# Moving the weight averages, one centring and one PSUM copy in a fused attention and convolution kernel

## The reference

```python
x = attention0(x)     # 1x1 projections q, k, v; softmax over 256 positions; gamma * out + x
x = attention1(x)     # the same form without the output projection
# layer 2: a pre-activation residual block with binary weights
out = relu(batch_norm(x, gamma0, beta0));  out = conv3x3(out, E0 * sign(w0))
out = relu(batch_norm(out, gamma1, beta1)); out = conv3x3(out, E1 * sign(w1)) + x
# layer 3: whitening across 4 groups of channels, then a 4x4 mix per channel
cov = perm @ perm.T / N + eps;  z = solve(cholesky(cov).T, perm);  y = weight @ z + bias
```

## Time and profile before

| | us |
|---|---|
| median of 3 runs | 70.65 |
| lowest and highest | 70.19, 70.87 |
| the profiled execution | 70.66 |
| its span, first to last instruction | 68.9 |

### The profile page before, as it was taken

One profiled execution on the slowest core, in us unless ns is written; L12 is line 12 of the kernel. 1 busy time (PEld: TensorE's weight loads), 2 busy tenths in 40 slices (PEclk: granted clock), 3 DMA queues, 4 the chain that ended last, 5 costly groups with the idle time before them and its releaser, 6 DMA issues.

```text
span 68.9 us, 1828 instructions
## 1 busy us (share of the span) xinstructions
PE 58.2 (85%) x654; PEld 34.6 (50%) x654; DVE 47.4 (69%) x129; ACT 43.0 (62%) x133; POOL 21.9 (32%) x59
## 2 busy tenths in 40 slices
PE   5997866839999899989695899979998999999910
PEld 2253531416364364445261457358974998774300
DVE  0029799487796987878699754677949969377440
ACT  0710498939989898989999593464008672455440
POOL 4001606860371817355303317470004050008200
PEclk9999999999999999999999999999999999999999
DMA  0889830000000000000000000000000000000025
GB/s 0 237 255 275 274 149 6 0 0 0 0 0 0 10 5 0 0 0 5 0 0 0 5 10 0 0 0 10 0 0 0 0 10 10 0 0 0 0 102 202
DMA packets 2168, 2.69 MB, mean 39 GB/s; under 512 B 368, under 2 KB 1520, under 8 KB 2160
## 3 DMA queue, kind: packets, MB, share of 16 engines
q1 hardware_dynamic: 1872, 2.39, 10.9%
q10 hardware_dynamic: 288, 0.20, 0.9%
HBM read 2.06 MB, written 0.52 MB: 37 GB/s over the span
## 4 chain that ended last, share of the span: by engine, by line
PE 54%; ACT 12%; DVE 11%; POOL 11%; issue 5%; POOLq 1%; DVEq 0%; ACTq 0%
PE bank L760 13%; PE bank L690 9%; ACT bank L458 8%; PE bank L590 6%; PE bank L600 5%; PE bank L624 4%; DVE cut L908 4%; PE bank L735 3%; PE bank L671 3%; POOL zn L405 2%; PE bank L656 2%; PE bank L661 2%; POOL cut L355 2%; POOL cut L358 2%; ACT hi L523 2%
## 5 line engine op out<-in xcount | busy, mean ns | idle before, releaser
L458 ACT ACTIVATE bank<-bank,negmax 128x256 f32<-128x256 f32 x32 | 14.3, 447 | 1.2 <-DVE negmax L898 1.0
L590 PE MATMUL bank<-const-bfloat16-1.0 128*128 128x512 bf16 x39 | 11.2, 419 | 0.8 <-PEq L1177 0.8
L898 DVE TENSOR_REDUCE negmax<-bank 128x2 f32<-128x512 f32 x16 | 10.4, 684 | 1.3 <-PE bank L640 1.3
L471 ACT ACTIVATE probs<-bank 128x512 f32<-128x512 f32 x16 | 8.6, 590 | 0.5 <-PE bank L661 0.5
L690 PE MATMUL bank<-probs,vt 128*64 128x256 f32 x64 | 8.7, 391 | 0.0
L908 DVE TENSOR_SCALAR cut<-bank,prm 128x256 f32<-128x256 f32 x8 | 3.9, 482 | 6.2 <-PE bank L600 6.1
L760 PE MATMUL bank<-hi,taps 64*64 64x225 f16 (+2 forms) x144 | 7.3, 267 | 0.8 <-ACT hi L523 0.8
L760 PE MATMUL bank<-lo,taps 64*64 64x225 f16 (+2 forms) x144 | 7.0, 265 | 0.0
L760 PEld LDWEIGHTS bank<-hi,taps 64*64 64x64 bf16 x144 | 6.0, 107 | 1.9 <-issue 0.9
L458 ACT ACTIVATION_READ_ACCUMULATOR bank<-bank,negmax 128x1 f32 x32 | 6.6, 205 | 0.0
L590 PEld LDWEIGHTS bank<-const-bfloat16-1.0 128*128 128x128 bf16 x39 | 3.9, 108 | 5.2 <-issue 2.5
(11 more groups left out here) (132 smaller groups left out, 101.6 us busy)
## 6 DMA issues: line engine op xcount, KB each, us to landing
cw<-conv_w SPq DMA_DIRECT2D x2, 288.0 KB, 4.6
x<-x_in SPq DMA_DIRECT2D x4, 128.0 KB, 2.7
out<-res SPq DMA_DIRECT2D x2, 256.0 KB, 2.1
kst<-consts SPq DMA_DIRECT2D x1, 428.0 KB, 5.6
aw<-attn_w ACTq DMA_DIRECT2D x1, 128.0 KB, 2.4
aw<-attn_w SPq DMA_DIRECT2D x1, 128.0 KB, 3.2
half<-select SPq DMA_DIRECT2D x1, 96.0 KB, 2.7
kst<-consts SPq DMA_DIRECT2D x1, 64.5 KB, 2.9
```

Of the source, the lines that this page charges most:

```text
L458: nc.scalar.activation(part, part, ACT.Exp, bias=negmax[:, i % 2, n:n + 1], accum_out=total[:, i % 2, n:n + 1]).then_inc(total_out, 1)
L471: nc.scalar.activation(probs[:, i % 2, g], pb_t[g][:].rearrange("p (t n) -> p t n", t=CH), ACT.Exp).then_inc(exp_out, 1)
L590: mm(bank[:], filler, filled, start=True, stop=True)
L898: ve.tensor_reduce(negmax[:, i % 2, g * CH:(g + 1) * CH], pb_s[(2 * i + g) % 3][:].rearrange("p (t n) -> p t n", t=CH), AX.X, ALU.max, neg ...
```

## The change

- PE takes the two averages of weights (L801) behind the second `combine` and ahead of `keep_warm`, no longer ahead of the first `combine`.
- DVE takes `emean` and `esq` behind the two `first_low` of convolution 0, no longer ahead of `bn_aggr`.
- `zn` of quarter 1 for the first norm is written by DVE right behind that of quarter 0; POOL's instruction and the semaphore `z_pool` are gone. `first_line(n, 0)` waits for both `zn` in both norms.
- The third of the four copies of transposes (`yt`, q = 2) is made by DVE, ahead of `sum_all`; ACT makes the other three. `gram(2)` waits for DVE's copy.

```diff
@@ POOL
                 pool.wait_ge(var_out, n + 1)
-                if n == 0:
-                    nc.gpsimd.tensor_scalar(zn[0][:, 1], xs[LAYERS][:, quarter(1)], mv[0][:, 0:1], bn_t[0][:, 4:5],
-                                            ALU.subtract, ALU.mult).then_inc(z_pool, 1)
                 pool.wait_ge(rstd_out, n + 1)
@@ ACT
-                    act.wait_ge(z_out, 1 if n == 0 else q + 2)
-                    if n == 0 and q == 1:
-                        act.wait_ge(z_pool, 1)
+                    act.wait_ge(z_out, 2 * n + q + 1)
...
-            for q in range(PAIRS):
+            for q in (0, 1, 3):
                 act.wait_ge(yt_mm, q + 1)
@@ PE
-                pe.wait_ge(yt_out, q + 1)
+                if q == 2:
+                    pe.wait_ge(yt_dve, 1)
+                else:
+                    pe.wait_ge(yt_out, (1, 2, None, 3)[q])
...
             pe.wait_ge(kst_in, 16)
+            pe.wait_ge(x_out, ITERS - 1)
+            pe.wait_ge(stats0_out, PAIRS - 1)
+            combine(0, range(PAIRS - 1))
+            pe.wait_ge(last_stats, 1)
+            combine(0, range(PAIRS - 1, PAIRS))
             pe.wait_ge(wabs_out, 2)
             for n in range(2):
                 last = mm(pb_mean[:, n:n + 1], kst[:, K_ONES:K_ONES + P], wabs[n][:],
                           start=True, stop=True)
             last.then_inc(e_mm, 1)
-            pe.wait_ge(x_out, ITERS - 1)
-            pe.wait_ge(stats0_out, PAIRS - 1)
-            combine(0, range(PAIRS - 1))
-            pe.wait_ge(last_stats, 1)
-            combine(0, range(PAIRS - 1, PAIRS))
             keep_warm(WARM[1], pb_q)
...
-            pe.wait_ge(z_out, 2)
+            pe.wait_ge(z_out, 3)
@@ DVE
             for n in range(2):
-                if n == 0:
-
-                    dve.wait_ge(e_mm, 1)
-                    step(ve.tensor_copy(emean[:], pb_mean[:, 0:2]))
-                    step(ve.tensor_tensor(esq[:], emean[:, 0:1], emean[:, 0:1], ALU.mult))
                 dve.wait_ge(comb_mm, n + 1)
...
-                for q in range(1 + n):
+                for q in range(2):
...
-                dve.wait_ge(z_out, 2 * n + 1)
                 dve.wait_ge(rstd_out, n + 1)
+                dve.wait_ge(z_out, 2 * n + 2)
                 first_line(n, 0)
                 if n == 0:
-                    dve.wait_ge(z_pool, 1)
                     first_line(0, 1)
                     first_low(0, 0)
                     first_low(0, 1)
+                    dve.wait_ge(e_mm, 1)
+                    step(ve.tensor_copy(emean[:], pb_mean[:, 0:2]))
+                    step(ve.tensor_tensor(esq[:], emean[:, 0:1], emean[:, 0:1], ALU.mult))
                     step(ve.tensor_scalar(esq[:], esq[:], E_SQUARE_MIN, None, ALU.max))
...
+            dve.wait_ge(yt_mm, 3)
+            ve.tensor_copy(yt[:, 4:6], pb_yt[2][:, 0:2 * P].rearrange("p (k g c) -> p k g c", k=2, g=G)).then_inc(yt_dve, 1)
             dve.wait_ge(yc_out, PAIRS)
```

More of the change, by code:

```diff
@@ L249, in build @@
         line_out, lo_out, lnvar_out = sem("line_out"), sem("lo_out"), sem("lnvar_out")
-        conv_mm, stats_out, z_out, z_pool = sem("conv_mm"), sem("stats_out"), sem("z_out"), sem("z_pool")
+        conv_mm, stats_out, z_out = sem("conv_mm"), sem("stats_out"), sem("z_out")
         act_sum_out = sem("act_sum_out")
@@ L254, in build @@
         xc_pool = sem("xc_pool")
-        yt_mm, yt_out = sem("yt_mm"), sem("yt_out")
+        yt_mm, yt_out, yt_dve = sem("yt_mm"), sem("yt_out"), sem("yt_dve")
         gram_mm, cov_out, cov_mm = sem("gram_mm"), sem("cov_out"), sem("cov_mm")
```

## The result

| | before | changed |
|---|---|---|
| median, us (20 runs each) | 70.77 | 70.17 |
| lowest | 70.19 | 69.68 |
| ratio of the times, 95% interval | | 0.9923 (0.9904 to 0.9942) |

The changed kernel is faster by 0.77%, 0.55 us. That is within the 1% that I called no change, and inside the range; the interval excludes no gain at all. Some runs of every kernel, the profiled one of the changed kernel among them (71.6 us, span 69.8), are a microsecond or more longer than the rest, and the ratios are made without those.

What follows compares the result with a forecast made beforehand. POOL's centring of quarter 1 was taken to set the paired steps' start; after the change DVE's chain binds, worth 0.64, with the third copy at 0. Forecast 70.66 - 0.6 = 70.05 us, range 69.65 to 70.6.

Steps and rivals of the forecast that it cites:

- Combining ahead of the averages: First norm: bn_aggr starts 0.70 behind the last statistics' end, at 43.13 instead of 43.48, a gain of 0.35 us.
- Centring by VectorE: Convolution 0: with quarter 1's zn on DVE, paired steps start at 45.45 instead of 46.08, 0.63 us gained so far.
- The stall at the first paired step: Convolution 0, before the change: quarter 1's first tap was expected at 45.80 but came at 46.08, 0.28 us of stall.
- step 6: Convolution 0: product step beside which quarter 1's first tap would go, at 45.80 in the kernel before.
- What VectorE pays: Convolution 0: DVE's rows run without a gap; second CAST ends at 47.41, matmul resumes at 47.49 instead of 48.13, worth 0.64.
- step 24: Convolution 0: product step beside which quarter 3's first tap goes, behind the second CAST; a 0.13 us stall was to stay.
- ACT and POOL hidden: Convolution 0: act32 of quarter 2 ends about 45.7, wanted by DVE at 46.26: 0.5 us of slack, or 0.15 with POOL waits.
- the slow rival: First norm: POOL's three small instructions begin only when DVE goes idle; 0.83 us lost, 71.5 us; chance 0.07.
- POOL's 1.37: First norm: POOL's zn of quarter 1 took 1.37 us, against 0.48 for its 128 x 256 instruction where DVE was idle.
- Third copy: End part: PE's Gram products, not ACT's copies, set the end; taken as 0, bounds 0.05 us gained and 0.15 lost.
- Sum: Whole kernel: 70.66 - 0.6 = 70.05 us for the profiled execution.

Runs made afterwards that it cites:

- a kernel whose first `act` comes 0.17 sooner behind S: Changed kernel with small VectorE instructions behind both CASTs and VectorE's waits moved; end 26.42 us behind the last bn_stats' start, timed ratio 0.9913.

## Why the prediction was right, step by step

- **Combining ahead of the averages: right in kind, 0.10 too large.** Forecast 0.35 at `bn_aggr`, measured 0.25. I took the 0.70 of the second norm for the idle time, but the first had two more semaphores to wait for; moving these gave 0.70 at once. The averages' products stayed covered: convolution 0 starts 1.69 behind `bn_aggr` in both kernels.
- **Centring by VectorE: right.** The stall at the first paired step went. Forecast 0.63 earlier, measured 0.76 (3.32 against 4.08), as the stall was 0.51 and not 0.28. I had put quarter 1's first product 0.63 behind the convolution's start, beside step 6; without a stall it starts 0.40 behind it. The mistake changed nothing in the sum, since VectorE's chain set the end of the stage: TensorE reached the next wait earlier and lost more there, 0.39 where I had 0.13.
- **What VectorE pays: right in mechanism, and too small in size.** The forecast had VectorE's chain bind at step 24, with the second CAST 0.64 earlier; it was 0.51. The missing 0.13 comes from the 0.10 above and 0.07 at the first `act`, which started 0.11 behind the second `zn`'s end and not 0.04, less 0.04 by which the rows behind it stood closer than forecast.
- **What I did not draw from it:** if VectorE's chain binds, then the 0.25 won at `bn_aggr` is paid back by `emean` and `esq` on that chain (two instructions 0.19 apart, 0.38). The centring alone gives 0.54 and the averages nothing on top. My text booked the two parts one after the other and never asked what each is worth without the other.
- **ACT and POOL hidden: right here.** 0.6 of slack was left. But the slow rival's mechanism is real and near: in the one trace of it, it cost 0.4 in a kernel whose first `act` comes 0.17 sooner behind S (2.32 against 2.49).
- **POOL's 1.37 read as waiting for VectorE: wrong.** Of the 0.88 above the 0.48 that I compared it with, 0.67 is the price of a subtract in this instruction on POOL, 0.07 that of a second scalar from a tile, and 0.14 is open. The forecast did not rest on it, since the instruction was removed.
- **Third copy: right,** 0.01.
- **Sum:** 0.6 forecast, 0.51 by the trace, 0.55 by the runs (0.77% of 70.77).

## What to carry to other kernels

When two engines are close behind each other, price each part of a change also alone and last: a part that starts the stage earlier is worth nothing if it puts its own length on the chain that binds later. Count time from an event just ahead of the change: here stages of the same form agreed within 0.02 us, and so told apart parts that a few timed runs could not. But one trace can catch an accident, as the 0.58 was, and a gain seen in stages alone still wants many timed runs. And put small instructions that nobody wants soon (here `emean` and `esq`) behind those that another engine waits for: by the stages this placing alone was worth 0.27 us, half as much again as the whole change brought.

## What the runs showed of the hardware

- A POOL `tensor_scalar` of 128 x 256 fp32 with subtract and multiply took 1.36 us, with add and multiply 0.69 in the same place, and VectorE took 0.41 for the former.
- POOL instructions of one element per partition took 0.19 us where they began up to 0.07 behind the start of VectorE's `act` (12 of 12), and 0.24 to 0.58 where they began 0.10 to 0.21 behind that of an `act` or `lo` (26 of 26); the long ones end 0.05 behind the end of an instruction of VectorE. VectorE's instructions kept their 0.41 to 0.43 beside them.
- A semaphore that was long met still cost 0.07 to 0.10 us ahead of an instruction on VectorE where it left the late one to an instruction of its own (`bn_aggr` at 1.23 against 1.13, `act` 0.11 against 0.04 behind `zn`). With the late one on the instruction itself the second cost nothing that these traces show.
